# A new first guess for the top-p search, two PSUM banks for the diffusion tiles of the head, and an earlier place for the exponentials of group 1

## The reference

```python
R = S / clip(S.sum(axis=1), 1e-12)         # S = adj + I
for s in range(2):
    A = _adj_from_feats(Xa, W1, W2, W3)    # 2048 x 2048
    Xf = R @ Xf                            # diffusion
    Xa = A @ Xa                            # attention
    Z = Z + (Xf @ U1s[s] + Xa @ U2s[s])
# _adj_from_feats: logits = Xa W1 W2 (Xa W3)^T; per row, softmax, sort, keep the
# largest entries until their sum passes 0.9 (top-p), softmax of what is kept
```

## Time and profile before

| | |
|---|---|
| median of 3 runs | 1469.48 us (1467.57 to 1470.49) |
| the profiled execution | 1471.02 us, span 1469.2 us |
| mean granted TensorE clock | 0.971 of full speed |
| TensorE / VectorE / ScalarE / GpSimd busy | 85% / 77% / 41% / 20% |

### The profile page before, as it was taken

How to read it: one execution, slowest core, us unless ns; L and a number is a source line. 1 busy time by engine, 2 the same in 40 slices (tenths; PEclk the granted TensorE clock), 3 DMA queues, 4 the chain that set the end, 5 groups by cost and what they waited for, 6 DMA issues and landing times.

```text
span 1469.2 us, 18872 instructions
## 1 busy us (share of the span) xinstructions
PE 1254.1 (85%) x6522; PEld 614.5 (42%) x6522; DVE 1126.0 (77%) x1916; ACT 601.0 (41%) x1137; POOL 289.2 (20%) x235
## 2 busy tenths in 40 slices
PE   0348999997699899989989899699989989999894
PEld 0123555553244445445445444234444444444442
DVE  6984666562799999899979900599599999779666
ACT  1331444444831345554354343850154354353331
POOL 4311343432132212112112201011101101021111
PEclk9878999999899999999999999999999999999998
DMA  6123454442134401211010230524412121020344
GB/s 208 57 86 152 174 197 173 184 157 86 44 114 130 134 23 58 72 51 65 22 59 29 67 129 29 187 80 134 131 63 72 37 80 49 32 72 29 96 153 175
DMA packets 53332, 142.86 MB, mean 97 GB/s; under 512 B 5312, under 2 KB 5312, under 8 KB 48896
## 3 DMA queue, kind: packets, MB, share of 16 engines
q1 hardware_dynamic: 53248, 141.86, 27.8%
HBM read 90.72 MB, written 51.12 MB: 97 GB/s over the span
## 4 chain that ended last, share of the span: by engine, by line
PE 62%; DVE 19%; ACT 9%; issue 7%; POOL 2%; DVEq 1%; ACTq 0%; POOLq 0%
PE AB L763 11%; PE RB L725 11%; PE UB L625 7%; PE AB L766 6%; DVE WS L1237 5%; PE RB L727 5%; PE AB L615 4%; PE AB L608 3%; PE RB L625 2%; ACT squares L948 2%; PE XB L625 2%; PE TB L634 2%; PE LB L698 2%; PE LB L699 2%; ACT E L941 1%
## 5 line engine op out<-in xcount | busy, mean ns | idle before, releaser
L1237 DVE SCALAR_TENSOR_TENSOR WS<-E,g 128x2048 bf16<-128x2048 f32 x144 | 343.9, 2440 | 1.3
L763 PE MATMUL AB<-XR,turns 128*128 128x512 f16 x1024 | 242.9, 380 | 0.0
L725 PE MATMUL RB<-VR,turns 128*128 128x512 f16 x1024 | 231.5, 379 | 0.0
L1324 DVE TENSOR_REDUCE g<-E 128x1 f32<-128x2048 f32 x32 | 72.9, 2279 | 106.0 <-ACT E L941 106.0
L725 PEld LDWEIGHTS RB<-VR,turns 128*128 128x128 f16 x1024 | 99.8, 98 | 113.9
L763 PEld LDWEIGHTS AB<-XR,turns 128*128 128x128 f16 x1024 | 100.1, 98 | 106.6 <-issue 2.4
L766 PE MATMUL AB<-XR,turns 128*128 128x512 f16 x512 | 131.4, 379 | 0.0
L519 POOL TENSOR_TENSOR RT<-RT,AD 128x512 f32<-128x512 f32 x32 | 56.8, 1775 | 377.5 <-ACT RT L983 377.5
L1007 ACT ACTIVATE turns<-TB 128x512 f16<-128x512 f32 x128 | 75.4, 594 | 126.6 <-PE TB L640 126.5
L727 PE MATMUL RB<-VR,turns 128*128 128x512 f16 x512 | 117.1, 379 | 0.0
L625 PE MATMUL UB<-UW,XT 128*128 128x512 f16 x384 | 88.2, 379 | 27.4 <-ACT XT L893 27.3
(11 more groups left out here) (256 smaller groups left out, 1969.1 us busy)
## 6 DMA issues: line engine op xcount, KB each, us to landing
turns<-adj_parts SPq DMA_DIRECT2D x64, 512.0 KB, 3.7
E<-adjT SPq DMA_DIRECT2D x16, 1024.0 KB, 5.0
adj_parts<-turns SPq DMA_DIRECT2D x16, 1024.0 KB, 3.8
z_d<-UO SPq DMA_DIRECT2D x31, 256.0 KB, 2.0
XR<-x SPq DMA_DIRECT2D x4, 1024.0 KB, 11.9
WS<-U SPq DMA_DIRECT2D x4, 1024.0 KB, 5.4
x_d<-E SPq DMA_DIRECT2D x16, 256.0 KB, 2.6
xu_d<-UO SPq DMA_DIRECT2D x16, 256.0 KB, 2.0
```

Of the source, the lines that this page charges most:

```text
L725: i = mm(RB[:, :], AT[:, 0, j, :], VR[:, j, k % 2, :], start=False, stop=False)
L763: mm(AB[:, :], ET[:, 0, j, :], XR[:, j, y_, :], start=(j == 0 and y_ == 0), stop=False)
L1237: return v.scalar_tensor_tensor(junk[t % 2], e, g4[:, k, t:t + 1], e, op, ALU.mult, accum_out=g4[:, F_, t:t + 1])
```

## The change

Three things:

1. **First guess.** ScalarE's exponential of the guess (L972), its buffer u0 and the semaphores s_lnu and s_u0 are gone. VectorE makes the exponential from the bits of the number instead. In step 0 the guess uses the row sums of the exponentials, so `search` there waits for all four exponentials of its group before its first pass; in step 1 it needs none of them. SEARCH is (4, 4) instead of (5, 4), OVERSHOOT (1.2, 1.2) instead of (1.4, 1.2).
2. **Two banks.** The diffusion tiles 0 to 8 go to AB and RB in turn (tile 0 in AB, 1 in RB, ..., 8 in AB). Tiles 1 to 9 wait only until the tile before the previous one is carried out. The first product of the pairs waits until tile 8 is out of AB.
3. **Order.** The terms of group 1 come between tile 6 and tile 7 of the head's loop, instead of behind tile 8. SyncE's sequence of transfers stays what it was.

```diff
-SEARCH = (5, 4)
+SEARCH = (4, 4)
-OVERSHOOT, CAP = (1.4, 1.2), (2.0, 0.5)
+OVERSHOOT = (1.2, 1.2)
+R_EARLY = R_FIRST - 2
...
             r_tile(s)
             logits(s, 1)
-            r_tiles(s)
+            r_tiles(s, 1, R_EARLY)
+            terms(s, 1)
+            r_tiles(s, R_EARLY, R_FIRST)
             for g in range(NG):
-                if g + 1 < NG:
+                if 0 < g < NG - 1:
                     terms(s, g + 1)
...
-            def r_tiles(s):
-                with sp.Fori(1, R_FIRST + 1) as t:
+            def r_tiles(s, a, b):
+                with sp.Fori(a, b) as t:
                     at_hi_in(s, t)
                     at_lo_in(s, t)
                     ad_in(s, t)
                     r_store(s, t - 1)
+                if b == R_FIRST:
+                    at_hi_in(s, b)
+                    at_lo_in(s, b)
+                    ad_in(s, b)
+                    r_store(s, b - 1)
...
-            def r_products(s, t, a, b):
+            def r_products(s, t, a, b, bank=RB, ahead=False):
...
-                        pe.wait_ge(s_re, r + OPEN)
+                        pe.wait_ge(s_re, r - (1 if ahead else 0) + OPEN)
...
-                r_products(s, 0, 0, R_ALL)
-
-            def r_tiles(s):
-                with pe.Fori(1, R_FIRST) as t:
-                    r_products(s, t, 0, R_ALL)
+                r_products(s, 0, 0, R_ALL, AB)
+
+            def r_tiles(s, a, b):
+                with pe.Fori(a, b, 2) as t:
+                    r_products(s, t, 0, R_ALL, RB, True)
+                    r_products(s, t + 1, 0, R_ALL, AB, True)
...
                 pe.wait_ge(s_xf, n)
+                if g + i == 0:
+                    pe.wait_ge(s_re, R_FIRST + s * T + OPEN)
                 terms_product(qq, 0)
...
                     a(E[:, slot, :], E[:, slot, :], ACT.Exp, bias=nmx[:, slot:slot + 1],
                       accum_out=tot[:, slot:slot + 1]).then_inc(s_exp, 1)
-                    if t == 0:
-                        act.wait_ge(s_lnu, gq + 1)
-                        a(u0[:, :], g4[:, LNU, :], ACT.Exp).then_inc(s_u0, 1)
...
-                ct(v.tensor_tensor(row(A1), row(MEAN), row(VAR), ALU.add))
-                ct(v.scalar_tensor_tensor(row(A1), row(SIG), -Z_P / 2, row(A1), ALU.mult, ALU.add))
-                ct(v.tensor_tensor(row(A1), row(A1), nmx[:, sl], ALU.add))
-                v.tensor_scalar(row(LNU), row(A1), -CAP[s], None, ALU.min).then_inc(s_lnu, 1)
+                ct(v.tensor_tensor(row(MEAN), row(MEAN), nmx[:, sl], ALU.add))
+                if s == 0:
+                    ct(v.scalar_tensor_tensor(row(A1), row(SIG), -Z_P / 2, row(MEAN), ALU.mult, ALU.subtract))
+                    ct(v.tensor_scalar(row(LNU), row(A1), PER_E, -UNIT - 2 * LOG_N * 2.0 ** 23 + SKEW, ALU.mult, ALU.add))
+                else:
...
+                    ct(v.reciprocal(row(LNU), row(LNU)))
+                    ct(v.tensor_tensor(row(U), row(U), row(LNU), ALU.mult))
...
-                dve.wait_ge(s_u0, gq + 1)
-                ct(v.tensor_copy(row(U), u0[:, :]))
+                if s == 0:
+                    dve.wait_ge(s_exp, G * gq + G)
+                    ct(v.scalar_tensor_tensor(row(LNU), tot[:, sl].bitcast(I32), 2.0, row(LNU), ALU.mult, ALU.add))
+                    ct(v.tensor_scalar(row(U).bitcast(I32), row(LNU), UNIT - FLOOR * PER_E, UNIT - CAP[s] * PER_E,
+                                       ALU.max, ALU.min))
```

More of the change, by code:

```diff
@@ L28 @@
 LOG_N = 11
-OVERSHOOT, CAP = (1.4, 1.2), (2.0, 0.5)
+OVERSHOOT = (1.2, 1.2)
+PER_E = 2.0 ** 23 / np.log(2.0)
+UNIT = 127 * 2.0 ** 23
+CAP, FLOOR = (2.0, 0.5), 15 * np.log(2.0)
+SKEW = 0.0430 * 2.0 ** 23
 NEAR = 0.75
@@ L194, in build @@
                 "s_v", "s_ve", "s_vh", "s_vl", "s_vout", "s_pk", "s_pkc", "s_pklo")]
-        s_lf, s_lc, s_sq, s_max, s_exp, s_lnu, s_u0, s_any, s_kept, s_rden = [
-            sem(n) for n in ("s_lf", "s_lc", "s_sq", "s_max", "s_exp", "s_lnu", "s_u0", "s_any", "s_kept", "s_rden")]
+        s_lf, s_lc, s_sq, s_max, s_exp, s_any, s_kept, s_rden = [
+            sem(n) for n in ("s_lf", "s_lc", "s_sq", "s_max", "s_exp", "s_any", "s_kept", "s_rden")]
         s_tf, s_eh, s_ts, s_et, s_a = [sem(n) for n in (
@@ L524, in r_tile @@
                 r_sum(s, 0)
-            def r_tiles(s):
-                with pool.Fori(1, R_FIRST) as t:
+            def r_tiles(s, a, b):
+                with pool.Fori(a, b) as t:
                     r_sum(s, t)
@@ L722, in r_products @@
                     if k < 2:
-                        i = mm(RB[:, :], id_sa[:, :], VR[:, t, k, :], start=(k == 0), stop=False)
+                        i = mm(bank[:, :], id_sa[:, :], VR[:, t, k, :], start=(k == 0), stop=False)
                     elif k < R_HI:
-                        i = mm(RB[:, :], AT[:, 0, j, :], VR[:, j, k % 2, :], start=False, stop=False)
+                        i = mm(bank[:, :], AT[:, 0, j, :], VR[:, j, k % 2, :], start=False, stop=False)
                     else:
-                        i = mm(RB[:, :], AT[:, 1, j, :], VR[:, j, 0, :], start=False, stop=(k == R_ALL - 1))
+                        i = mm(bank[:, :], AT[:, 1, j, :], VR[:, j, 0, :], start=False, stop=(k == R_ALL - 1))
                     if k == R_HI - 1:
@@ L850, in r_behind @@
             def r_behind(s, t):
-                r_products(s, t, 0, R_ALL)
+                r_products(s, t, 0, R_ALL, ahead=(t == R_FIRST))
             step_order(0, logits, nothing, r_tile, r_tiles, pairs, r_behind)
@@ L969, in terms, with r_out @@
                       accum_out=tot[:, slot:slot + 1]).then_inc(s_exp, 1)
-                    if t == 0:
-                        act.wait_ge(s_lnu, gq + 1)
-                        a(u0[:, :], g4[:, LNU, :], ACT.Exp).then_inc(s_u0, 1)
-            def r_out(s, t):
+            def r_out(s, t, bank=RB):
                 r = t + s * T
@@ L982, in r_out @@
                     act.wait_ge(s_rout, 16 * t + OPEN)
-                a(RT[:, :], RB[:, :], ACT.Copy, scale=rinv[:, bass.ds(t, 1)]).then_inc(s_re, 1)
+                a(RT[:, :], bank[:, :], ACT.Copy, scale=rinv[:, bass.ds(t, 1)]).then_inc(s_re, 1)
                 if s == 0:
@@ L989, in r_tile, with r_tiles @@
             def r_tile(s):
-                r_out(s, 0)
-            def r_tiles(s):
-                with act.Fori(1, R_FIRST) as t:
+                r_out(s, 0, AB)
+            def r_tiles(s, a, b):
+                with act.Fori(a, b, 2) as t:
                     r_out(s, t)
+                    r_out(s, t + 1, AB)
             def e_hi(qq, c):
```

9 lines of the change are left out of this document (7 added, 2 removed).

## The result

The changed kernel takes 1475.47 us (median of 10 runs, 1474.78 to 1480.9) and the kernel before 1469.24 (10 runs, 1467.57 to 1473.49): ratio 1.0045, 95% interval 1.0033 to 1.0056. It is 6.2 us slower. 1468.7 was forecast, with a range that ended at 1474.5, and slower had a chance of 0.18.

A forecast was written before the change was run, and what follows sets the result against it. Bound by the heads and by places where ScalarE, in fixed order, waits for VectorE while TensorE waits for ScalarE. +7.0 - 3.4 - 3.9 - 0.5 = -0.8 us gives 1468.7; 8-in-10 range 1462.0 to 1474.5.

The forecast's parts named there:

- the load becomes the next thing that is late: Heads, two banks: a boundary gains 0.6 or 0.42 us, not 1.2, as the high half's load lands late; step 1 gains 3.4.
- the last rival: Heads: the clock falls between two-bank tiles, 16 restarts of 2.1 us make 34 us, 1502; chance 0.02.
- The search ended as the change says: Step 0: a rival said four iterations leave a row outside its window and bisection runs, about 1608; chance 0.04.
- the hold of tile 9: Step 0's head: moved exponentials delay tile 7's carry-out and store, so tile 9's load lands at 503.5, 4.9 us later.
- The restart at the lower clock: Step 0, tile 9: after about 10.5 us idle, ten products run at 0.43 instead of 0.216, 2.1 us more.
- the edit costed at nothing: Step 0's other groups: waiting for four exponentials adds 5.5 us to VectorE, hidden under the iteration that goes.
- the chain behind tile 7: Step 0's head: from carry-out to the store's issue 5.4 or 7.2 us, mostly by GpSimd's sum; 6.2 taken.
- So nothing is held: Step 1's head: tile 7's carry-out starts about when it did, so tile 9's load, due at 1054.5, isn't delayed.
- Group 2: Step 1, group 2: ScalarE no longer waits for the guess, so 3.9 us goes between diffusion tile and first product.
- The second logits of step 1: Step 1: one small exponential less ahead of the second logits, 0.5 us gained.
- the long hold: Slower rival: the iteration gives only 12.0, the chain takes 7.2, step 1's tile 9 is held too, 1473.9; chance 0.12.

The follow-up runs named there:

- the split load: The changed kernel with the load of the high half cut in two, first half issued after the 18th product: 1476.27 us; with the exponentials back behind tile 8, 1453.25.
- the last experiments: The change with exponentials back behind tile 8 and step 0's search of groups 2 and 3 held: 1461.52 us; with the load in two as well: 1449.32.
- VectorE held: The changed kernel with step 0's search, except group 1's, started only when ScalarE has made VHL of the diffusion tile beside it: 1474.65 us.

## Why the prediction was wrong

**Right: the load becomes the next thing that is late.** Periods of 11.4 and 11.57 were forecast; 11.5 (step 0) and 11.6 (step 1) came; the split load shows the cause. The clock between two-bank tiles did not fall, against the last rival: the granted clock is 1.00 from 402 to 490 us and from 976 to 1066. The search ended as the change says. The rule of the Trainium skill, "TensorE: Matmul & The Clock Gate", section "A second HAM failure mode: psum-queue depth-cycling", is shown by no run here.

**Right: the hold of tile 9, by its mechanism.** Exponentials, carry-out of 7, GpSimd, SyncE's order, load: each link stands in the rows, and SyncE's link was cut by itself. Its terms, set to a common start (these executions begin group 0 3.4 us apart): carry-out at 494.2 for 493.2 forecast, 5.3 us from there to the store for 6.2, load issued 0.57 behind it for 0.4 and landed in 4.2 for 3.7. Tile 9 came 5.8 late by that start and 4.9 was forecast; 1.1 of the 5.8 had arisen by the second logits already, so that the table has 4.7 for the rest. The restart at the lower clock cost 2.3 for 2.1.

**Wrong: the edit costed at nothing.** "The 5.5 us that the wait for four exponentials adds in the other groups of step 0 lies under the iteration that goes." As VectorE's own time that holds. What failed is that I asked only when VectorE ends and not beside whom it starts. By waiting, its passes move to the moment at which GpSimd adds, and it is GpSimd that ScalarE and TensorE wait for. That happened at three places: second logits +1.1 (sum 3.17 for 1.56, less 0.5 for the small exponential that goes), tile 12 +2.2 and tile 15 +1.0 (sum 3.17 for 2.28 at both). Together 4.3 us. A fourth meeting has another origin: behind tile 9, +2.5 (sum 2.40 for 1.27, wait 2.57 for 1.45, and a half-clock stretch that costs more than the wait). There the sum of the late tile 9 meets the last pass of the search's second iteration, and not its start. With the exponentials back behind tile 8 it meets the first passes instead and takes 2.81 us; no run isolates this place. The four make 6.8 us, of which none was forecast; they are most of the 8.7 by which the trace misses the forecast. The rows were at hand: the earlier trace rows have both durations, and I used them in the chain behind tile 7, where the short one came, and nowhere else. The rule of the Trainium skill that I weighed there ("GPSIMD Engine Reference", section on specifications) had its place in these four stretches: each has a sum of 2.40 or 3.17 us beside the passes.

The rows also divide the 6.8: TensorE's wait is longer by 1.1 at tile 9 and by 0.9 at tiles 12 and 15 each (3.37 for 2.49, 4.39 for 3.51), and the products behind it lose 1.4, 1.3 and 0.1 more at the lower clock. How much of it a kernel gets back is open, between 0 and 3.9 for tiles 12 and 15, by the last experiments.

**Mis-sized: step 1.** "So nothing is held; if I am 2 us off, each further microsecond costs one." I was 1.8 off: the last exponential ended at 1060.3 where 1058.5 is the forecast moved by the shift of that trace. The store of 7 went at 1063.04, the load behind it at 1064.15, and it took 4.6 instead of 3.8. That is 1.1 of the 3.4 us. Group 2 gave 3.5 of 3.9.

**Not foreseeable from the trace of before:** +1.4 from a half-clock stretch at 1379 to 1383 us (0.57, where before had 1.00) in a part without an edit; and the start of the profiled execution. I argued from 1471.02, an execution that was 3.4 us behind after's before the change could act (2.4 us in layer 0, 1.0 in the first logits). The second logits of step 1 gained 1.5 us where 0.5 was forecast; what gave the other 1.0 stays open.

**The rival that was right in sign** was the long hold, with 1473.9 and 0.12. But its mechanism isn't what happened: tile 9 was not late beyond the forecast. A hold near the forecast's size, with the meetings of GpSimd and VectorE that had no price, was enough. What the experiments add is its size: the hold and what it brings cost 13.8 us (1475.47 less 1461.63), against 7.7 that the other two parts give.

## What to carry to other kernels

- Before an instruction goes ahead of others on an in-order engine, ask when its own input comes. Here ScalarE stood 10.4 us idle in front of a finished tile, and a gain elsewhere (10.8 us a tile instead of 11.5) went into that wait to the last microsecond.
- A wait that costs its own engine nothing can still move its work beside a neighbour that shares something with it. For each added wait, look at which engines are busy in the stretch that the work now falls on, and who waits for them.
- Two parts of one change can need each other (banks and guess: -2.4 and +5.0 us alone, -7.7 together), and a third can hide that. One kernel with a single part undone said more than the sum of the parts alone.

## What the runs showed of the hardware

- **GpSimd's sum and VectorE's passes take turns here.** Over one 128x512 sum beside VectorE's passes, GpSimd shows 3.17 us at tiles 12 and 15, and 1.26 or 1.27 with VectorE held. At tile 12 the numbers fit a lock: the sum starts at 638.35 during a pass that ends at 640.4, and 2.0 + 1.26 is 3.3; the next pass then takes 3.34 instead of 2.35, and the low part, started at 642.25 in that pass, 2.43 instead of 1.15. The Trainium skill, "SBUF — State Buffer", section "SBUF: two separate sides", describes the shared pair as an exclusive lock, where the one that comes second "fully blocks"; these rows agree. An estimate from these rows: a GpSimd operation that starts beside unbroken passes waits for the rest of one pass, up to 2.35 us.
- **Short waits are followed by the lower clock too.** After a wait of 2.57 us, TensorE had 0.52 from 519.2 to 522.6, 3.4 us long; ten products in it cost 1.4 us more than in before, which had 1.45 us of wait there and no such stretch. Around the 9.66 us of wait it stood at 0.51 from 495.3 to 505.5: 5.7 us of that lie in the wait, and eleven products in the rest.
- **A load behind a late store lands later:** 4.2 and 4.6 us (tile 9 of either step) where the others of the head take 3.6 to 3.9. In step 0 the low half was issued 0.4 us behind it instead of 3.5, so there the store is not the only company; no run separates the two.
- **One large load in two, each half issued when its part of the buffer is free, hid all of it.** The Trainium skill, "Perfetto Trace Analysis", section "DMA Optimizations", says that smaller chunks may start sooner; here it was worth 7 to 8 us where nothing else held the tiles, and nothing where something did.
